# A new order of convolution units, evictions shared unit by unit, and a folded last chunk

## The chip, the cores and the metric

The kernel runs on one core of a Trainium2 chip. The metric is the device time of one execution in microseconds. Three runs of the kernel before took 3115.51, 3118.27 and 3122.56 us; the median is 3118.27.

The engines are TensorE (PE; matmuls), VectorE (DVE), ScalarE (ACT), GpSimd (POOL) and SyncE (SP, which issues the DMAs here). Each runs its own list of instructions in order and waits on semaphores.

## The reference

The input x has shape (8, 16, 112, 112): 8 images, 16 channels. Four residual stages follow each other, each on the group-normalised x (`_gn`: 8 groups of 2 channels, mean and variance over the group in the whole image):

```
x = x + L0(_gn(x))   # attention in windows of 4x4 pixels, 16 heads of width 1, projection
x = x + L1(_gn(x))   # 3x3 convolution, 16 -> 16 channels
x = x + L2(_gn(x))   # grid of 4 columns x 4 rows of 3x3 convolutions (below)
x = x + L3(_gn(x))   # 3x3 convolution of x rounded to 8 bits by one scale over all images
```

L2 is most of the work. Each of its 16 cells convolves up to three inputs of 16 channels and gives, after bias and relu, three outputs of 16 channels (right, up, down):

```
if col == 0:    ins = [input] if row == 0 else [outs[row - 1][-1]]
elif row == 0:  ins = [outs[row][0], outs[row + 1][1]]
elif row == 3:  ins = [outs[row][0], outs[row - 1][-1]]
else:           ins = [outs[row][0], outs[row + 1][1], outs[row - 1][-1]]
outs[row] = cell(W[col, row], b[col, row], ins)      # result: outs[-1][0]
```

L3's scale is the largest absolute value over all images, so L3 starts when the last image has left L2. In the attention of L0, each of the 16 queries of a window gets scores against 16 keys, a softmax over the keys and the weighted sum of the values.

## The kernel before

**Stages.** The program is written out as bodies m = -1 .. 7. Body m works on the grid of image m from cell (2,2) on, together with the first cells (columns 0, 1 and part of 2) of image m + 1, the attention of image m + 2 and conv1 (L1) of images m + 1 and m + 2. Ahead of body -1 (the early body, which has only the first cells of image 0) the attention of image 0 runs alone. Body 5 is the last with attention, body 6 (the late body) has convolutions alone, body 7 (the last) only the late cells of image 7. Then L3 runs for all images.

**Units.** A cell's outputs are computed unit by unit: 22U0 is cell (col 2, row 2), output up, first half of the image. `BODY` lists the cells, `units_of` takes all units of one cell one after the other. There are 68 in a body, 50 in the early, 18 in the last. In `conv_unit` (L846 for the last cell, L856, L870) a unit's matmuls go to two of four banks of PSUM. An input held as a "pair" (two inputs, 128 partitions) takes 48 matmul instructions at L856, one held as a "half" (64 partitions) 48 at L870. Cells of column 0 have a half alone, cells of rows 0 and 3 in the other columns a pair alone, the rest both. Unit k may start when unit k - 2 is emptied.

**Emptying** (eviction: bias and relu from PSUM into the input tiles of later cells). ScalarE does it in L706, four quarters per unit of 32x784 elements (or 32x392 twice, into a half). In cells that `SHARED_MID` names, which are (0,0) to (0,3), ScalarE takes two quarters and VectorE two (L1058, `empty`). The second half of an output emptied, SyncE sends its rows to the neighbouring partitions ("halos"): two DMAs for a pair (L497, L498), six for a half (L462 to L470). A unit's first use waits for them.

**Side steps** stand at fixed units, in tables: `PE_FIRST/MID/BEFORE` (attention's qkv L817 and projection L827, conv1 L783, the matmuls of means and variances L760, L765), `ACT_*` (copy of qkv L687, exponential L692), `SP_*` (loads, sends of the normalised input, store of a finished image). FIRST is body -1, BEFORE body 5, MID the bodies between. Both engines run their list in order, so a side step that must wait holds the units behind it.

**VectorE** in a body: the attention in 14 steps ("j"): `scores` (L1071 to L1083), `weigh` (L1095 to L1102), `residual` (L1110) after each projection; `add_conv1` (with the second normalising, L1046); `finish` of an image (L1267, added to the stream and measured); `move_stream`; `turn` at the end, with the statistics for the next image. Its evictions stand at fixed places: cell (0,0) after weigh 4, (0,1) after weigh 5, (0,2) after weigh 6, then `finish`, and (0,3) between scores 8 and weigh 7.

**First attention.** For image 0 a chunk's scores lie with the keys outermost, and TensorE sums over the 16 keys by matmuls with the identity (L890, `first_sums`): once the exponentials ("den"), once the weighted values ("num"). VectorE weighs (L1164), divides (`first_divide`, L1171, L1176) and adds the residual. There are 7 chunks.

## Time and profile before

| | us |
|---|---|
| median of three runs | 3118.27 |
| the profiled run | 3120.86 |
| its span, first to last instruction | 3119.1 |
| TensorE (PE) busy | 2786.1 (89%) |
| VectorE (DVE) busy | 2299.9 (74%) |
| ScalarE (ACT) busy | 2011.4 (64%) |
| mean granted clock of TensorE | 0.964 |

On the chain of waits that ended last TensorE has 70% of the span, VectorE 15%, ScalarE 10%. A row of the profile names the line of the kernel, the engine, the operation, output<-inputs and how often; a bracket at its end is the time that the engine was idle before it and what ended that. "Granted clock" 1.00 is 2.4 GHz, 0.50 is 1.2 GHz; there is nothing between the two but means over a stretch. An end of a matmul is modelled, so lengths of TensorE are best read from start to start.

### The profile page before, as it was taken

What the parts mean: (1) busy time and instruction counts of PE and PEld (TensorE: products, weight loads), DVE (VectorE), ACT (ScalarE), POOL (GpSimd) and SP (SyncE); (2) the same over time, 40 slices, a digit from 0 to 9 for tenths busy, and PEclk for the clock granted to TensorE, in tenths of its full rate; (3) what the DMA queues carried; (4) which work ended last, traced back from release to release, by engine and by line L of the source; (5) the groups of instructions that cost most, each with busy time, mean ns of one, the idle gap of its engine ahead of it and who ended that gap; (6) DMA issues with size and microseconds to landing.
All of it is one profiled execution on the core that took longest, in us unless ns stands there. A gap on an engine that the chain in (4) does not pass through costs nothing.

```text
span 3119.1 us, 84833 instructions
## 1 busy us (share of the span) xinstructions
PE 2786.1 (89%) x39155; PEld 1185.7 (38%) x39155; DVE 2299.9 (74%) x2105; ACT 2011.4 (64%) x2318; POOL 23.5 (1%) x68
## 2 busy tenths in 40 slices
PE   4755899989998899989998999989998989889976
PEld 3742333333333333333433343333333333333333
DVE  8969985899688986889598987899599961240135
ACT  1107976766767676766776776767776775766524
POOL 0000000000000000000000000000000000000000
PEclk9877999999999999999999999999999999999998
DMA  1014656586667667675657766685657664775566
GB/s 63 11 21 63 84 79 91 72 111 89 85 84 95 94 84 99 80 105 79 84 84 92 102 89 90 86 113 74 94 74 99 90 88 64 94 107 73 79 89 181
DMA packets 37555, 268.00 MB, mean 86 GB/s; under 512 B 19280, under 2 KB 19920, under 8 KB 24784
## 3 DMA queue, kind: packets, MB, share of 16 engines
q1 hardware_dynamic: 37008, 261.77, 59.6%
q8 instruction: 308, 5.05, 0.9%
q10 hardware_dynamic: 192, 0.80, 0.2%
q14 instruction: 47, 0.39, 0.1%
HBM read 22.54 MB, written 12.04 MB: 11 GB/s over the span
## 4 chain that ended last, share of the span: by engine, by line
PE 70%; DVE 15%; ACT 10%; issue 3%; SPq 1%; DMA 1%; POOL 0%; ACTq 0%; POOLq 0%; DVEq 0%
PE conv_banks L856 43%; PE conv_banks L870 20%; ACT pair L706 5%; ACT half L706 4%; DVE pair L1058 2%; DVE half L1058 2%; PE side_banks L817 2%; PE stat_bank L827 1%; PE side_banks L783 1%; ACT scores L692 1%; PE conv_banks L954 1%; DMA half<-half 1%; DVE scores L1073 1%; DVE score_max L1081 1%; DVE scores L1071 1%
## 5 line engine op out<-in xcount | busy, mean ns | idle before, releaser
L706 ACT ACTIVATE pair<-conv_banks,b_cells 32x784 f32<-32x784 f32 x1316 | 1213.0, 922 | 586.9 <-PE conv_banks L870 520.0
L856 PE MATMUL conv_banks<-pair,w_cells 128*32 128x392 f32 x17664 | 1538.1, 497 | 25.2 <-issue 11.6
L870 PE MATMUL conv_banks<-half,w_cells 64*32 64x392 f32 x18432 | 880.2, 508 | 143.8 <-ACT pair L706 60.7
L856 PEld LDWEIGHTS conv_banks<-pair,w_cells 128*32 128x32 f32 x17664 | 559.6, 109 | 948.0 <-issue 904.3
L706 ACT ACTIVATE half<-conv_banks,b_cells 32x392 f32<-32x392 f32 (+1 forms) x780 | 520.4, 667 | 172.7 <-PE conv_banks L870 133.9
L870 PEld LDWEIGHTS conv_banks<-half,w_cells 64*32 64x32 f32 x18432 | 337.4, 107 | 666.6 <-issue 620.8
L1058 DVE TENSOR_SCALAR half<-conv_banks,b_cells 32x392 f32<-32x392 f32 (+1 forms) x180 | 114.4, 636 | 326.5 <-PE conv_banks L870 168.4
L1058 DVE TENSOR_SCALAR pair<-conv_banks,b_cells 32x784 f32<-32x784 f32 x220 | 227.5, 1034 | 109.3 <-PE conv_banks L870 99.1
L1071 DVE TENSOR_TENSOR scores<-qkv 128x1792 f32<-128x1792 f32 x98 | 197.8, 2019 | 71.8 <-ACT qkv L687 71.5
L692 ACT ACTIVATE scores<-scores 128x1792 f32<-128x1792 f32 x104 | 176.7, 1699 | 78.5 <-DVE scores L1155 46.1
L1097 DVE TENSOR_TENSOR scores<-scores,qkv 128x1792 f32<-128x1792 f32 x98 | 198.4, 2025 | 3.4
L1073 DVE TENSOR_TENSOR scores<-scores,rel_bias_sb 128x1792 f32<-128x1792 f32 x98 | 198.4, 2025 | 3.3
L1083 DVE TENSOR_TENSOR scores<-scores,score_max 128x1792 f32<-128x1792 f32 x98 | 198.4, 2025 | 3.3
L1100 DVE TENSOR_REDUCE score_max<-scores 128x112 f32<-128x1792 f32 x98 | 197.9, 2020 | 3.4
L1081 DVE TENSOR_REDUCE score_max<-scores 128x112 f32<-128x1792 f32 x98 | 197.9, 2020 | 3.4
L1095 DVE TENSOR_REDUCE softmax_sum<-scores 128x112 f32<-128x1792 f32 x98 | 197.2, 2012 | 0.4
L687 ACT ACTIVATE qkv<-side_banks 128x672 f32<-128x672 f32 x56 | 40.9, 731 | 122.3 <-PE side_banks L817 92.5
L1046 DVE TENSOR_SCALAR half<-stream,norm 32x784 f32<-32x784 f32 x128 | 87.1, 680 | 3.1 <-DVE norm L1012 0.2
L1098 DVE RECIPROCAL softmax_sum<-softmax_sum 128x112 f32<-128x112 f32 x98 | 82.8, 845 | 0.0
L846 PE MATMUL conv_banks<-pair,w_cells 128*32 128x392 f32 x768 | 70.0, 515 | 12.5 <-issue 11.7
L817 PE MATMUL side_banks<-att,w_qkv_sb 128*128 128x224 f32 x294 | 68.0, 369 | 9.1 <-DVE att L1031 9.1
L827 PE MATMUL stat_bank<-att,w_proj_sb 128*128 128x112 f32 x448 | 65.8, 291 | 10.7 <-DVE stream L1110 10.7
(107 smaller groups left out, 1042.3 us busy)
## 6 DMA issues: line engine op xcount, KB each, us to landing
pair<-pair SPq DMA_DIRECT2D x384, 391.9 KB, 8.6
half<-half SPq DMA_DIRECT2D x348, 192.4 KB, 5.6
x_block<-in_xa SPq DMA_DIRECT2D x8, 784.0 KB, 11.0
stream<-in_xs SPq DMA_DIRECT2D x8, 784.0 KB, 10.5
x_scratch<-stream SPq DMA_DIRECT2D x7, 784.0 KB, 6.9
pair<-x_scratch SPq DMA_DIRECT2D x7, 784.0 KB, 14.2
out_dram<-pair SPq DMA_DIRECT2D x4, 1120.0 KB, 5.3
half<-half SPq DMA_DIRECT2D x174, 7.1 KB, 4.7
```

Of the source, the lines that this page charges most:

```text
L692: nc.scalar.activation(e, e, ACT.Exp).then_inc(exp_done, 1)
L706: done = nc.scalar.activation(dst, src, ACT.Relu, bias=b_ap)
L856: done = nc.tensor.matmul(conv_ps[32 * q:32 * q + 32, n + b, 0:QN], w, P[row][:, QG * s + BG * (q // 2):QG * s + BG * (q // 2 + 1), BX * ( ...
L870: done = nc.tensor.matmul(conv_ps[32 * q:32 * q + 32, n + h, 0:QN], w_all[rows, at:at + 32], T[rows, QG * u + BG * (q // 2):QG * u + BG * ...
L1058: done = nc.vector.tensor_scalar(dst, src, b_ap, 0.0, ALU.add, ALU.max)
L1071: ch.inc(nc.vector.tensor_tensor(e4, q, key, ALU.mult))
L1073: ch.inc(nc.vector.tensor_tensor(e, e, relb[:].unsqueeze(1).to_broadcast([BP, SW, WPX * WPX]), ALU.add))
L1081: ch.inc(nc.vector.tensor_reduce(m[:], ea, AX.X, ALU.max))
L1083: nc.vector.tensor_tensor(ea, ea, row_max(m), ALU.subtract).then_inc(scores_ready, 1)
L1095: side.inc(nc.vector.tensor_reduce(den[:], ea, AX.X, ALU.add))
L1097: side.inc(nc.vector.tensor_tensor(e4, e4, v, ALU.mult))
L1100: side.inc(nc.vector.tensor_reduce(mx[:], ea, AX.X, ALU.add))
```

## The change

- The list of cells is replaced by a list of units, `ORDER`, in which units of different cells alternate. A star marks units of the late cells. The early body runs those without a star, the last body those with one.
- VectorE's share of the evictions is given unit by unit: `VEC_MID` names 16 units at three places of VectorE's list (after weigh 4, after scores 7, after weigh 6), `VEC_LATE` 36 units of body 6, `VEC_LAST` 6 units of body 7. `finish` goes behind scores 10, `move_stream` behind weigh 13 (behind scores 2 in the early body).
- All tables of side steps get other places.
- In the early body `add_conv1` goes ahead of the first scores.
- In the first attention the last chunk's weighted values are added up by VectorE in four halving steps instead of by TensorE, and the division is split into `first_invert` and `first_apply`, placed ahead of the next weighing. The wait of the cleared tiles (GpSimd) is for one sum less.
- The first image's two normalised inputs are written half by VectorE, half by ScalarE.

```
-BODY = [((3, 0), 1), ((2, 2), 1), ((3, 1), 1), ((2, 3), 1), ((0, 0), 0), ((3, 2), 1), ((0, 1), 0), ((3, 3), 1),
-        ((0, 2), 0), ((1, 0), 0), ((0, 3), 0), ((1, 1), 0), ((1, 2), 0), ((2, 0), 0), ((1, 3), 0), ((2, 1), 0)]
-EARLY_BODY = [x for x in BODY if not x[1]]
-LATE_BODY = [x for x in BODY if x[1]]
...
+ORDER = """
+22U0* 22U1* 22D0* 22D1* 30D0* 30D1* 22R0* 22R1* 23U0* 23U1* 31D0* 31D1* 00D0 00D1 23R0* 00R0 23R1*
+32D0* 32D1* 00R1 01D0 01D1 01R0 01U0 01U1 33R0* 33R1* 02U0 02U1 01R1 02D0 10D0 02D1 02R0 02R1 10D1
+10R0 10R1 03U0 03U1 11U0 11D0 11D1 11U1 11R0 11R1 03R0 03R1 12D0 12D1 20D0 12U0 12U1 12R0 12R1 20D1
+20R0 20R1 13U0 13U1 13R0 13R1 21D0 21U0 21D1 21U1 21R0 21R1
+"""
...
+UNITS = units(ORDER)
+UNITS_F = [unit(t) for t in ORDER.split() if t[4:] != "*"]
+UNITS_L = [unit(t) for t in ORDER.split() if t[4:] == "*"]
...
+PE_MID = {0: [("qkv", 1, 0)], 4: [("proj", 0, 0), ("qkv", 2, 0)], 12: [("proj", 1, 0)], 13: [("qkv", 3, 0)],
+          19: [("proj", 2, 0)], 20: [("qkv", 4, 0)], 39: [("proj", 3, 0), ("qkv", 5, 0)],
+          47: [("proj", 4, 0), ("qkv", 6, 0)], 52: [("proj", 5, 0)], 56: [("proj", 6, 0)],
+          58: [("mean1", 0, 0)], 59: [("var1", 0, 0), ("mean0", 0, 1)], 60: [("var0", 0, 1)],
+          62: [("qkv", 0, 1)], 63: [("conv1", 0, 1)], 64: [("conv1", 1, 1)], 65: [("mean2", 0, 1)],
+          66: [("var2", 0, 1)]}
...
+PE_BEFORE = {0: [("qkv", 1, 0)], 4: [("proj", 0, 0), ("qkv", 2, 0)], 12: [("proj", 1, 0)], 13: [("qkv", 3, 0)],
+             19: [("proj", 2, 0)], 20: [("qkv", 4, 0)], 39: [("proj", 3, 0), ("qkv", 5, 0)],
+             47: [("proj", 4, 0), ("qkv", 6, 0)], 52: [("proj", 5, 0)], 56: [("proj", 6, 0)],
+             58: [("mean1", 0, 0)], 59: [("var1", 0, 0)], 63: [("conv1", 0, 1)], 64: [("conv1", 1, 1)],
              65: [("mean2", 0, 1)], 66: [("var2", 0, 1)]}
...
+ACT_MID = {0: [("qkv", 1, 0), ("exp", 1, 0)], 3: [("exp", 2, 0)], 5: [("qkv", 2, 0)], 6: [("exp", 3, 0)],
+           10: [("exp", 4, 0)], 14: [("qkv", 3, 0)], 16: [("exp", 5, 0)], 18: [("exp", 6, 0)],
+           24: [("qkv", 4, 0)], 25: [("exp", 7, 0)], 39: [("exp", 8, 0)], 41: [("qkv", 5, 0)],
+           43: [("exp", 9, 0)], 45: [("exp", 10, 0)], 48: [("qkv", 6, 0)], 49: [("exp", 11, 0)],
+           52: [("exp", 12, 0), ("exp", 13, 0)], 61: [("qkv", 0, 1)], 62: [("exp", 0, 1)]}
...
+SP_FIRST = {0: [("xb", 1), ("input", 0)], 30: [("xa", 2)], 38: [("conv1", 1)], 40: [("xb", 2)],
+            47: [("input", 1)]}
+SP_MID = {49: [("x3", -1), ("xa", 2)], 59: [("conv1", 1)], 62: [("xb", 2)], 65: [("input", 1)]}
+SP_BEFORE = {49: [("x3", -1)], 59: [("conv1", 1)], 65: [("input", 1)]}
+SP_LATE = {49: [("x3", -1)]}
+SP_LAST = {4: [("last", 0)], 13: [("last", 1)], NL - 2: [("last", 2)]}
...
+VEC_FIRST = {}
+VEC_MID = {("w", 4): "31D1 00D0 00D1 23R0",
+           ("s", 7): "01D0 01D1 01R0 01U0 01U1",
+           ("w", 6): "02U0 02U1 01R1 02D0 10D0 02D1 02R0"}
+FINISH_AT = ("s", 10)
+MOVE_AT_FIRST, MOVE_AT = ("s", 2), ("w", 13)
+VEC_LATE = """22U0 22D0 22D1 30D0 22R0 22R1 23U0 31D0 31D1 00D0 00D1 23R0 32D1 00R1 01D0 01D1 01R0 01U0 01R1 02D0
+10D0 02D1 02R0 02R1 10R0 10R1 03U0 11U0 11D1 11R0 11R1 03R0 12D0 12R0 12R1 13U1"""
+VEC_LAST = """22D1 30D1 31D0 31D1 23R1 32D1"""
+
+SHARED_FIRST, SHARED_MID = [[u for text in at.values() for u in units(text)] for at in (VEC_FIRST, VEC_MID)]
+SHARED_LATE, SHARED_LAST = units(VEC_LATE), units(VEC_LAST)
...
+                act.wait_ge(norm_sems[1 + which]["norm_ready"], 1)
+                for q in range(2, NQ):
+                    lo = QG * (q % 2)
+                    for xh in range(2):
+                        at = slice(32 * swapped(q, xh), 32 * swapped(q, xh) + 32)
+                        done = nc.scalar.activation(
+                            S[INPUT[1]][64:96, lo:lo + QG, 1 + BX * xh:1 + BX * (xh + 1)],
+                            X[at, :, BX * xh:BX * (xh + 1)], ACT.Identity, bias=nm[at, 3:4], scale=nm[at, 2:3])
+                    done.then_inc(c_own, 1)
+                act.wait_ge(c_own, (which + 1) * 2)
...
+                last = k == WROWS - 1
+                if k >= 1 and not last:
                     first_num(k - 1)
-                if k >= 2:
+                if k >= 2 and not last:
                     side_step(-2, "proj", k - 2)
                 pe.wait_ge(exp_done, SUBS * (k + 1))
...
+            side_step(-2, "proj", WROWS - 3)
             first_num(WROWS - 2)
-            first_num(WROWS - 1)
...
+                alone = not (isinstance(i, int) and i == 0)
+                for q in range(NQ if alone else 2):
...
+            def empty(m, mine):
+
+                for cell, o, u in mine:
+                    k = units_in(m).index((cell, o, u))
...
+            def first_fold(k, n):
+
+                dve.wait_ge(first_weighted, k + 1)
+                first.wait()
+                e = first_chunk_E[k % 3]
+                first.inc(nc.vector.tensor_tensor(e[:, 0:n], e[:, 0:n], e[:, n:2 * n], ALU.add))
...
+                    if 1 <= k < WROWS - 1:
+                        first_invert(k - 1)
+                        first_apply(k - 1)
+                    if k < WROWS - 1:
+                        first_weigh(k)
+                    if 2 <= k < WROWS - 1:
                         residual(0, k - 2)
-                first_divide(WROWS - 1)
-                residual(0, WROWS - 2)
+                k = WROWS - 1
+                first_invert(k - 1)
+                residual(0, k - 2)
+                first_weigh(k)
+                first_fold(k, 8)
+                first_apply(k - 1)
+                for n in (4, 2, 1):
+                    first_fold(k, n)
+                first_invert(k)
+                first_apply(k)
+                residual(0, k - 1)
...
+            def other_work(m, at):
+
+                early = isinstance(m, int) and m < 0
+                empty(m, units((VEC_FIRST if early else VEC_MID).get(at, "")))
+                if at == FINISH_AT and not early:
+                    finish(m, m)
+                if at == (MOVE_AT_FIRST if early else MOVE_AT):
+                    move_stream(m + 1)
...
+            def late_body(m):
+
+                mine, end = shared_in(m), units_in(m).index((LAST, RIGHT, 1))
+                before = [u for u in mine if m == B - 1 or units_in(m).index(u) < end]
+                if m < B - 1:
+                    add_conv1(m + 1)
+                empty(m, before)
+                finish(m, m)
+                empty(m, mine[len(before):])
+                if m < B - 1:
+                    move_stream(m + 1)
...
+                if early:
+                    add_conv1(m + 1)
                 scores(i, 0, side, E[:, 0], mx)
-                add_conv1(m + 1)
+                other_work(m, ("s", 0))
+                if not early:
+                    add_conv1(m + 1)
+                other_work(m, ("c1", 0))
                 for j in range(NSUB):
                     if j % SUBS == 0 and j // SUBS + 1 < WROWS:
                         normalise_chunk(i, j // SUBS + 1)
                     if j + 1 < NSUB:
                         scores(i, j + 1, side, E[:, (j + 1) % 2], mx)
-                    if not early and j == 7:
-                        empty(m, [(0, 3)])
+                        other_work(m, ("s", j + 1))
                     weigh(i, j)
-                    if not early and j == 4:
-                        empty(m, [(0, 0)])
-                    if not early and j == 5:
-                        empty(m, [(0, 1)])
-                    if not early and j == 6:
-                        empty(m, [(0, 2)])
-                    if not early and j == 6:
-                        finish(m, m)
-                    if j == 9:
-                        move_stream(m + 1)
+                    other_work(m, ("w", j))
```

## Rows read from the trace of the kernel before

**Rows 1.** Windows by stage: length, busy us of PE, PEld, DVE, ACT, POOL; granted clock, DMA.

```profile
247.70:531.50 283.80, 242.22 (x3464) 97.53 (x3464) 230.13 (x191) 218.66 (x257) 1.65 (x3) 0.93 0.56 78
531.50:2254.20 1722.70, 1631.62 (x24070) 657.11 (x24070) 1453.21 (x1286) 1230.62 (x1415) 8.23 (x15) 0.99 0.66 90
1910.30:2254.20 343.90, 325.22 (x4822) 131.07 (x4814) 290.70 (x258) 246.13 (x283) 1.65 (x3) 1.00 0.67 91
2254.20:2609.30 355.10, 328.59 (x4816) 130.25 (x4810) 280.26 (x242) 244.99 (x283) 1.10 (x2) 0.97 0.63 85
2609.30:2932.90 323.60, 306.42 (x4611) 116.16 (x4612) 53.17 (x64) 216.26 (x262) 0.00 (x0) 0.99 0.66 87
2932.90:3051.60 118.70, 100.78 (x1344) 41.91 (x1344) 33.98 (x36) 33.67 (x40) 1.59 (x6) 0.91 0.64 97
```

**Rows 2.** Groups by line and shape, one middle body: busy, mean ns, idle before and releasers.

```profile
L856 PE MATMUL conv_banks<-pair,w_cells 128*32 128x392 f32 x2208 | 192.3, 496 | 2.5 <-ACT half L706 1.3 <-issue 0.7 <-DVE pair L1058 0.5
L706 ACT ACTIVATE pair<-conv_banks,b_cells 32x784 f32<-32x784 f32 x164 | 151.2, 922 | 68.7 <-PE conv_banks L870 60.9 <-PE conv_banks L856 5.9
L870 PE MATMUL conv_banks<-half,w_cells 64*32 64x392 f32 x2312 | 107.8, 500 | 15.5 <-ACT pair L706 6.9 <-DVE half L1058 6.3 <-ACT pair L703 1.3
...
L1058 DVE TENSOR_SCALAR pair<-conv_banks,b_cells 32x784 f32<-32x784 f32 x28 | 29.0, 1034 | 7.1 <-PE conv_banks L870 6.7
...
L1046 DVE TENSOR_SCALAR half<-stream,norm 32x784 f32<-32x784 f32 x17 | 11.6, 680 | 0.4
L817 PE MATMUL side_banks<-att,w_qkv_sb 128*128 128x224 f32 x42 | 9.4, 359 | 0.0
...
L827 PE MATMUL stat_bank<-att,w_proj_sb 128*128 128x112 f32 x56 | 8.0, 286 | 0.0
...
L783 PE MATMUL side_banks<-half,w_conv 64*32 64x392 f32 x96 | 4.4, 490 | 0.0
```

**Rows 3.** Timeline of TensorE in the same body: start, length, what, idle before.

```profile
1926.07 4.20 PE L856 MATMUL conv_banks<-pair,w_cells 128*32 128x392 f32 x48
...
1932.35 4.20 PE L856 MATMUL conv_banks<-pair,w_cells 128*32 128x392 f32 x48
...
2025.96 4.34 PE L870 MATMUL conv_banks<-half,w_cells 64*32 64x392 f32 x96 [0.36 <-issue]
...
2053.56 5.60 PE L870 MATMUL conv_banks<-half,w_cells 64*32 64x392 f32 x96 [4.53 <-DVE half L1058]
...
2064.02 16.20 PE L856 MATMUL conv_banks<-pair,w_cells 128*32 128x392 f32 x192 [0.20 <-DVE pair L1058]
```

**Rows 4.** Timeline of VectorE in the same body, at the evictions of unit (0,2).

```profile
2035.58 2.02 DVE L1071 TENSOR_TENSOR scores<-qkv 128x1792 f32<-128x1792 f32 x1
...
2050.91 5.13 DVE L1058 TENSOR_SCALAR half<-conv_banks,b_cells 32x392 f32<-32x392 f32 x8
```

**Rows 5.** Timeline of body 5 at conv1, TensorE's and SyncE's rows.

```profile
2557.81 3.04 SPq L462 DMA_DIRECT2D half<-half  x1
...
2572.91 4.18 PE L783 MATMUL side_banks<-half,w_conv 64*32 64x392 f32 x48 [7.68 <-DMA half<-half]
```

**Rows 6.** Timeline of TensorE in the late body: a stall without a releaser.

```profile
2797.05 1.50 PE L870 MATMUL conv_banks<-half,w_cells 64*32 64x392 f32 x10 [4.41 <-issue]
```

**Rows 7.** Timeline of TensorE in the last body.

```profile
3013.59 6.83 PE L856 MATMUL conv_banks<-pair,w_cells 128*32 128x392 f32 x48 [6.22 <-issue]
...
3040.51 11.05 PE L846 MATMUL conv_banks<-pair,w_cells 128*32 128x392 f32 x96 [11.66 <-issue]
```

**Rows 8.** Timeline at the end of the first attention, VectorE and TensorE.

```profile
174.35 6.92 PE L890 MATMUL conv_banks<-scores,identity 128*128 128x224 f32 x32
...
181.30 3.89 DVE L1164 TENSOR_TENSOR scores<-scores,qkv 128x3584 f32<-128x3584 f32 x1 [8.91 <-PE conv_banks L890]
...
193.46 0.39 DVE L1176 TENSOR_TENSOR att<-conv_banks,pair 128x224 f32<-128x224 f32 x1 [3.84 <-PE conv_banks L890]
```

**Rows 9.** Timeline of VectorE at the end of the early body's attention.

```profile
461.90 0.45 DVE L1110 SCALAR_TENSOR_TENSOR stream<-stat_bank,b_proj_sb,stream 128x224 f32<-128x224 f32 x1 [8.54 <-PE stat_bank L827]
```

More of the change, by code:

```diff
@@ L105, in strips_of, with unit, units, starts @@
     return (u, u + 2) if has_single(col, row) else (2 * u, 2 * u + 1)
-BODY = [((3, 0), 1), ((2, 2), 1), ((3, 1), 1), ((2, 3), 1), ((0, 0), 0), ((3, 2), 1), ((0, 1), 0), ((3, 3), 1),
-        ((0, 2), 0), ((1, 0), 0), ((0, 3), 0), ((1, 1), 0), ((1, 2), 0), ((2, 0), 0), ((1, 3), 0), ((2, 1), 0)]
-EARLY_BODY = [x for x in BODY if not x[1]]
-LATE_BODY = [x for x in BODY if x[1]]
-def units_of(body):
-    return [(cell, o, u) for cell, late in body for o in cell_outs(*cell) for u in range(2)]
-UNITS_F, UNITS, UNITS_L = units_of(EARLY_BODY), units_of(BODY), units_of(LATE_BODY)
+ORDER = """
[4 more added lines that the diff above has]
+"""
+def unit(text):
+    return (int(text[0]), int(text[1])), "RUD".index(text[2]), int(text[3])
+def units(text):
+    return [unit(t) for t in text.split()]
+UNITS = units(ORDER)
+UNITS_F = [unit(t) for t in ORDER.split() if t[4:] != "*"]
+UNITS_L = [unit(t) for t in ORDER.split() if t[4:] == "*"]
 NF, NB, NL = len(UNITS_F), len(UNITS), len(UNITS_L)
 NS = NF + (B - 1) * NB + NL
-def body_of(m):
-    return (EARLY_BODY if m < 0 else LATE_BODY if m == B - 1 else BODY) if isinstance(m, int) else BODY
 def units_in(m):
-    return units_of(body_of(m))
+    return (UNITS_F if m < 0 else UNITS_L if m == B - 1 else UNITS) if isinstance(m, int) else UNITS
+def starts(m, k):
+    done = units_in(m)
+    return done[k][0] not in [cell for cell, _, _ in done[:k]]
 def unit_base(m):
@@ L153, in count_halos @@
             wrote(m, "input", INPUT)
-        for (cell, late) in body_of(m):
-            need[m, cell] = [(key, n[key]) for key in in_places(*cell)]
-            for o in cell_outs(*cell) if cell != LAST else []:
+        for k, (cell, o, u) in enumerate(units_in(m)):
+            if starts(m, k):
+                need[m, cell] = [(key, n[key]) for key in in_places(*cell)]
+            if u == 1 and cell != LAST:
                 wrote(m, (cell, o), out_place(*cell, o))
-        if m == -1:
-            n_first = dict(n)
     return need
@@ L226, in n_shared @@
 def n_shared(m, end):
-    return sum(cell in shared_in(m) for cell, _, _ in units_in(m)[:end])
+    return sum(done in shared_in(m) for done in units_in(m)[:end])
 def vec_value(m, k):
-    ahead, per = n_shared(-1, NF), sum(cell in SHARED_MID for cell, _, _ in UNITS)
+    ahead, per = n_shared(-1, NF), len(SHARED_MID)
     if not isinstance(m, int):
@@ L704, in empty @@
                     return
-                for dst, src, b_ap in unit_operands(k, cell, o, u, range(2 if cell in shared_in(m) else NQ)):
+                for dst, src, b_ap in unit_operands(k, cell, o, u, range(2 if (cell, o, u) in shared_in(m) else NQ)):
                     done = nc.scalar.activation(dst, src, ACT.Relu, bias=b_ap)
@@ L880, in body @@
                         side_step(m + d, kind, j)
-                    if cell == (0, 0) and cell != seen:
+                    if cell == (0, 0) and starts(m, k):
                         wait_halos(pe, m, "input")
-                    conv_unit(m, k, cell, o, u, cell != seen).then_inc(conv_done, 1)
-                    seen = cell
+                    conv_unit(m, k, cell, o, u, starts(m, k)).then_inc(conv_done, 1)
             def first_sums(kind, k, done_sem):
@@ L1048, in normalise_stream @@
                             nm[at, 2:3], nm[at, 3:4], ALU.mult, ALU.add)
-                    done.then_inc(c_ready, 1)
-            def empty(m, cells):
-                for k, (cell, o, u) in enumerate(units_in(m)):
-                    if cell not in cells:
-                        continue
+                    done.then_inc(c_ready, 1 if alone else 2)
+            def empty(m, mine):
+                for cell, o, u in mine:
+                    k = units_in(m).index((cell, o, u))
                     dve.wait_ge(conv_done, unit_base(m) + k + 1)
@@ L1336, in _ @@
             body(B - 3)
-            body(B - 2)
-            body(B - 1)
+            late_body(B - 2)
+            late_body(B - 1)
             dve.wait_ge(main_chain, B * MAIN_CHAIN)
```

105 lines of the change are left out of this document (37 added, 68 removed).

## The prediction, made before the changed kernel had run

> **What bounds the kernel now.** The windows by stage come first [rows 1]. The five middle bodies (one body is one image's 68 units) take 1722.7 us, 344.5 each; in the one shown TensorE is busy for 325.2 of 343.9, VectorE for 290.7, ScalarE for 246.1. So TensorE sets the pace there, and what can be won are its gaps. The same body by line and shape [rows 2] prices them: idle before the convolution's matmuls is 2.5 + 15.5 = 18.0, released by evictions of ScalarE and VectorE. TensorE's rows in order of time [rows 3] give clean prices: a unit with both inputs takes 6.28 from start to start (1926.07 to 1932.35), one with a pair alone 4.04 (16.20 for four), one with a half alone 2.1 to 2.2 (4.34 for two). A body has 28, 18 and 20 of these and two of the last cell at about 4.1: 175.8 + 72.7 + 42 + 8.2 = 298.7. Side steps cost 9.4 + 8.0 + 4.4 [rows 2] less some overlap, so a body without a gap is some 320. The other 24 are waits (18.0), half units started at 2.23 after a wait instead of 2.09, and loss of clock: after the wait of 4.53 two half units take 5.60 instead of 4.34 [rows 3].
>
> Why the waits stand where they do: two units share four banks, so unit k needs the eviction of k-2. A pair's eviction costs ScalarE 4 x 0.92 = 3.7, or with VectorE on two quarters about 2.1 (2 x 1.03) [rows 2]. The old order runs the short half units in blocks of four to six, each shorter than its eviction. And VectorE must be there: it ended an attention step (scores 8.1, weighing 7.2; 15.3 from 2035.58 to 2050.9) before it could begin on unit (0,2) [rows 4], which is the wait of 4.53.
>
> **The change, part by part.**
>
> *Order and evictions of a middle body.* TensorE's work is the same; only waits move. VectorE takes 16 units a body instead of 20, so 8 quarters go to ScalarE: +7.4 there, which has 98 idle, and -8 on VectorE. I ran the order by hand with these prices, from the body's start. VectorE begins the body's second step about 5 before it, since conv1 and its statistics stand two units and one unit earlier. Its first stop (after weighing 4) then comes at -5 + 77 = 72; TensorE finishes that stop's first unit, 31D1, at 70. This costs waits of 0.6, 0.35 and 0.25. At the second stop (after scores 7) VectorE is ready at 108.2 and TensorE ends its first unit at 107.5: waits 0.9, 0.3, 0.35. At the third (after weighing 6) VectorE is ready at 127.2 and the unit ends at 129.9, so it is VectorE that waits, 2.7. Then 1.25 behind the last cell (it is emptied only when both halves are done, as before) and 0.2 to 0.35 five times. Later: 1.3 at the fourth projection (VectorE's residual ends at 163.6, TensorE is there at 162.4) and 1.15 at 12D0. Between blocks the half units now stand among units of 4.04 and 6.28, during which ScalarE's 3.7 is hidden. Together 7.7, against 18.0. What was hidden and could become late: the seventh projection, at 260; VectorE's last weighing, the stream's move (now behind it) and a residual end at 258.9. That cover is 1.4 thin. To the 320 I add 7.7, 1 for conv1 (below) and 3.5 for the slower start after a wait: 332, or 12.5 less per body, 62.6 for five. Bounds: with no wait left it would be 320 (-24); if each of the three stops cost what one costs today (4.5 and 1.3 of clock), 332 + 17 = 349 (+5). I take 332, since the hand run stands on rows for every duration.
>
> *A rule against it.* ScalarE evicts 32x784 in 0.922 us, VectorE in 1.034 [rows 2]. The Trainium skill (ScalarE: Activation LUTs, Rules for kernel authors) says the opposite, that relu belongs on VectorE; by that, giving 8 quarters back to ScalarE would lose. The trace disagrees for this shape. And by either price the sum stays, because ScalarE is not the bound.
>
> *conv1 two units earlier.* Its halos are sent after the input is normalised, behind the second variance step, which moves up two units also; those are pair units (4.04), the ones it passes are long (6.28), so conv1 has some 4.5 less time after the normalising. Before, it starts with no wait (idle 0.0, L783 [rows 2]); after, SyncE takes this send ahead of two pair sends that stood before it. I take 1; bounds 0 and the 7.7 seen in body 5. In body 5 conv1's sends went out from 2557.81, right behind the pair sends of 13R1, and landed 15.1 later; TensorE waited 7.68 [rows 5]. The new table lets SyncE stand at conv1 three units earlier and places conv1 17 to 18 behind the variance step instead of 16.6, so I let this wait go. Body 5: 355.1 to 329.5, or -25.5 (waits as in the others -12.5; the wait at conv1, a second one behind it and their slow clock -13). Bounds -8 (halos stay late) and -34.
>
> *The late body (image 6).* No attention runs, VectorE takes 36 units instead of 20. By hand from 31D1 to 11U0: 92.4 against 82.8 of work; the largest waits are 1.8 and 1.5 at 01R1 and 02D0, when VectorE still adds and measures the finished image, and 1.2 behind the last cell. That gives 298.7 + 9.6 + 2. Not all of before's excess are evictions: a stall of 4.41 has no releaser [rows 6] and I leave half of such stalls in. 323.6 to 312.6: -11, bounds 0 and -18.
>
> *The last body.* TensorE waits 6.22 before 32D0 and then runs that pair part in 6.83 instead of 4.2 [rows 7]: the pair send of 23U stood behind a load of the scratch stream. Now 23U is four units ahead of 32D0 and that load goes out later. What is late next is 31D's half send, with the 8.1 of 23R and the 4.1 of 32D's own pair part before it; it needs about 11.6 and just fits. -8, bounds 0 and -9. The 11.66 before the last cell stays.
>
> *First attention.* VectorE waits 8.91 for the sixth chunk's sum over keys and 3.84 for the weighted sum [rows 8]; TensorE had three blocks of sums to run there, the first in 6.92. The fold replaces the last block by four VectorE additions of 3360 elements in all: up to 3.9, the price of the 3584-element multiply beside it [rows 8]. New path: sum of keys at 177 (its wait now ends when att 4 is applied, 168), weighing to 182.4, fold and apply to 187, reciprocal and product to 189.0, where the last product ended at 193.85: -4.9, and -0.4 for the residual behind it, which no longer meets TensorE's queue: -5.3. Dividing the normalising by two engines takes 4 of 8 instructions of 0.68 [rows 2] off VectorE but adds 4 of about 0.92 on ScalarE (an estimate, from its evictions of that shape), whose sends follow them: 5.4 becomes 3.7 to the last halo, -1.7. conv1 before the first scores: a further -5 for TensorE, since its sums no longer stand behind 8.1 of scores. The first conv unit could so start at 236 instead of 247.7 [rows 1]; yet ScalarE, in its order, stands at the third exponential until VectorE's scores are there, and VectorE's own chain has gained only some 6. So of 12 about 6 count.
>
> *The early body.* Its 50 units are 42 + 48.5 + 113 of work at the prices above, with side steps 223; it takes 283.8 [rows 1], since ScalarE empties everything. In the new order two of the half units and 10D, 10R stand between longer ones. By hand VectorE, 14 steps of 15.3, becomes the pace: attention ends at 444 (453.4 before, where VectorE then waited 8.54 for TensorE [rows 9]); projection 6 at 445, then 65 of work to the end at 511. I take 512 against 531.5: -19.5 with the part before. Bounds -8 and -24.
>
> **Sum.** 19.5 + 62.6 + 25.5 + 11 + 8 = 126.6 from the profiled run's 3120.9 (span 3119.1): 2994. The median of the runs shown is 2.6 below that run. For waits that such a hand run doesn't see (about half a microsecond a body) I add 5: 2997.
>
> **Rivals.**
> 1. VectorE is the second bound. The cover of 1.4 at the last projection is gone if anything makes VectorE late, and then every lateness is paid by TensorE. For it: 290.7 - 8 busy and the waits at norms stay. Against: the stops themselves ask for under 8. Half of the middle gain, two thirds elsewhere: 3120.9 - 31 - 43 = 3047.
> 2. Halos late at conv1: six bodies at 4 to 5 and 1.3 of clock: +30, 3027. For: the wait of 7.68. Against: the queue is empty when the send goes out.
> 3. Slower: VectorE comes late at all three stops. Unit k+2 waits on its half, and SyncE, in order, holds every later halo. The price of one late stop is on record: 4.53 and 1.3. It decides from 18 a body (126.6 over seven), which is 6 a stop; at 7 a stop the time is 3120.9 - 127 + 147 = 3141. For: VectorE was late at (0,2). Against: the hand run has it 2.2 late, 0.7 late and 2.7 early.
> 4. The order changes nothing since halos, not evictions, release the units: against it, the releasers [rows 2] are evictions, and DMA is none of them.
>
> The clock: TensorE is granted 1.00 in the body shown and 0.93 in the early one [rows 1]. The Trainium skill (TensorE: Matmul & The Clock Gate, Part 1) has idle time throttle the clock to half; the 5.60 after 4.53 agrees. By it, the short waits of the new order lose no clock, as the sum above has it too, and those of rival 3 do.
>
> **How the numbers follow.** Forecast 0.72, rival 1 0.12, rival 2 0.09, rival 3 0.05, rival 4 0.02. Own range of the forecast 2970 to 3025 (the bounds of the parts, with several at one side). The range to hold 8 in 10 reaches into rivals 1 and 2: 2968 to 3043. About 0.2% (6 us) is what a measurement can tell here: faster 0.93, same 0.02, slower 0.05.
>
> **What would show it.** Middle bodies near 332, with no wait of TensorE over 2; VectorE's evictions at the three stops begin within 3 of their unit's end; conv1 of body 5 with no DMA wait; 32D0 in the last body without its 6.22; the early body ending near 512. Wrong it would be if bodies stayed at 340 or more, above all with the wait at projections 3 or 6, or at conv1.

## The result, and the profile after

The changed kernel takes 3032.27 us (median of four runs, 3028.12 to 3042.12), 0.9731 of the kernel before (95% interval 0.9715 to 0.9747), 84.6 less than the 3116.89 that are the median of the kernel before with a fourth run (3113.03) counted in. The forecast was 2997, or 121 less. The time lies in the stated range of 2968 to 3043, but 35 above the forecast and outside the forecast's own range of 2970 to 3025. The profiled run has a span of 3030.6.

The windows by stage of the changed kernel (columns as in [rows 1]): the early body, the five middle bodies (0 to 4), the last of these alone (body 4), body 5, the late body, the last body.

```profile
236.30:516.20 279.90, 241.43 (x3475) 97.29 (x3477) 243.29 (x199) 220.78 (x259) 1.65 (x3) 0.94 0.57 79
516.20:2198.20 1682.00, 1627.84 (x24071) 660.22 (x24070) 1416.46 (x1256) 1265.80 (x1446) 8.25 (x15) 1.00 0.68 93
1862.10:2198.20 336.10, 325.90 (x4815) 131.75 (x4814) 283.31 (x252) 253.16 (x290) 1.65 (x3) 0.99 0.68 93
2198.20:2529.00 330.80, 322.91 (x4799) 129.71 (x4798) 265.19 (x231) 249.63 (x286) 1.10 (x2) 1.00 0.67 88
2529.00:2853.10 324.10, 307.30 (x4617) 117.34 (x4609) 87.55 (x102) 186.41 (x224) 0.00 (x0) 0.99 0.68 89
2853.10:2962.00 108.90, 97.22 (x1352) 35.98 (x1344) 13.29 (x16) 52.68 (x60) 1.59 (x6) 0.95 0.70 104
```

| stage | before | forecast | after |
|---|---|---|---|
| end of the early body | 531.5 | 512 | 516.2 |
| five middle bodies | 1722.7 | 1660 (332 each) | 1682.0 (339.8, 334.3, 332.8, 339.0, 336.1) |
| body 5 | 355.1 | 329.5 | 330.8 |
| late body | 323.6 | 312.6 | 324.1 |
| last body | 118.7 | 110.7 | 108.9 |

So the gain is missing in two stages: 22 in the middle bodies and 11.5 in the late body, which gained nothing in this trace. These are the groups of body 4 that answer to [rows 2]:

```profile
L891 PE MATMUL conv_banks<-pair,w_cells 128*32 128x392 f32 x2208 | 191.1, 496 | 1.9 <-ACT pair L741 1.4 <-DVE pair L1092 0.3 <-DVE half L1092 0.2
L741 ACT ACTIVATE pair<-conv_banks,b_cells 32x784 f32<-32x784 f32 x177 | 163.3, 922 | 51.3 <-PE conv_banks L905 42.6 <-PE conv_banks L891 6.4
L905 PE MATMUL conv_banks<-half,w_cells 64*32 64x392 f32 x2304 | 108.5, 501 | 5.4 <-DMA half<-half 2.5 <-ACT pair L741 1.0 <-issue 0.8
...
L1092 DVE TENSOR_SCALAR pair<-conv_banks,b_cells 32x784 f32<-32x784 f32 x16 | 16.5, 1034 | 10.1 <-PE conv_banks L905 8.1 <-PE conv_banks L891 1.8
```

The wait of 18.0 before the convolution's matmuls is now 7.3. VectorE's three stops there, and TensorE's rows that answer to [rows 3, 4]:

```profile
1932.55 7.77 DVE L1092 TENSOR_SCALAR half<-conv_banks,b_cells 32x392 f32<-32x392 f32 x12
...
1968.42 5.13 DVE L1092 TENSOR_SCALAR half<-conv_banks,b_cells 32x392 f32<-32x392 f32 x8
...
1993.72 2.09 DVE L1092 TENSOR_SCALAR pair<-conv_banks,b_cells 32x784 f32<-32x784 f32 x2 [6.31 <-PE conv_banks L905]
```

```profile
1989.80 5.13 PE L905 MATMUL conv_banks<-half,w_cells 64*32 64x392 f32 x80 [2.55 <-DMA half<-half]
...
2028.71 1.12 PE L862 MATMUL stat_bank<-att,w_proj_sb 128*128 128x112 f32 x8 [1.45 <-DVE stream L1144]
...
2078.53 4.19 PE L891 MATMUL conv_banks<-pair,w_cells 128*32 128x392 f32 x48 [1.36 <-ACT pair L741]
```

The first unit of the first stop, 31D1, ends at 1930.83 and that of the second, 01D0, at 1967.62; VectorE is 1.7 and 0.8 late (forecast 2 and 0.7). The fourth projection waits 1.45 (1.3), 12D0 1.36 (1.15). At the third stop VectorE waits 6.31 for 02U0 (forecast 2.7), because that unit itself is late: TensorE stood 2.55 for a DMA, and its 48 matmuls and 32 of the next unit's then took 5.13, where 96 take 4.34 in [rows 3]. The wait of 4.53 in front of the same unit before the change [rows 3] is back with another releaser. The waits of all five middle bodies (time in total, how often, the longest):

```profile
PE conv_banks L891 <- ACT pair L741: 10.0, 8, 1.4
PE conv_banks L905 <- issue: 8.4, 6, 3.1
PE conv_banks L905 <- DMA half<-half: 7.6, 3, 3.1
PE conv_banks L905 <- ACT pair L741: 5.1, 5, 1.0
PE conv_banks L891 <- issue: 4.8, 4, 1.7
PE conv_banks L905 <- DVE half L1092: 4.3, 13, 0.5
PE stat_bank L862 <- DVE stream L1144: 3.1, 3, 1.5
```

Evictions have 19.4 in these rows, 4 a body. The 13.2 of "issue" (no releaser in the trace) and the 7.6 of DMA were not among the forecast's waits. In the late body (TensorE) the same two stand:

```profile
2644.04 8.59 PE L881 MATMUL conv_banks<-pair,w_cells 128*32 128x392 f32 x78 [3.17 <-issue]
...
2701.35 2.49 PE L905 MATMUL conv_banks<-half,w_cells 64*32 64x392 f32 x48 [2.07 <-DMA half<-half]
...
2713.61 1.53 PE L905 MATMUL conv_banks<-half,w_cells 64*32 64x392 f32 x7 [3.52 <-issue]
```

**What the two are.** 02U0 needs the halos of 01D. SyncE's rows around it:

```profile
1964.75 0.51 SPq L521 DMA_DIRECT2D pair<-pair  x1
...
1968.50 0.51 SPq L521 DMA_DIRECT2D pair<-pair  x1
...
1973.58 0.83 SPq L486 DMA_DIRECT2D half<-half  x1
...
1979.22 0.93 SPq L494 DMA_DIRECT2D half<-half  x1
```

The send of 01D's half starts at 1973.58 and its last part goes out at 1979.22, behind the pair sends of 32D (1964.75) and 00R (1968.50); the landing of the last part was at 1989.71, 16.1 after the first issue. The windows of that stretch and three others show why (the last three columns are granted clock, DMA share and GB/s):

```profile
1969.00:1987.20 18.20, 17.11 (x288) 6.76 (x272) 17.52 (x19) 12.16 (x16) 0.00 (x0) 1.00 1.07 134
1990.50:1993.00 2.50, 2.50 (x40) 0.94 (x32) 0.00 (x0) 0.00 (x0) 0.00 (x0) 0.50 0.13 17
2080.00:2084.00 4.00, 4.00 (x68) 1.58 (x65) 3.70 (x4) 2.85 (x4) 0.00 (x0) 1.00 0.89 98
2632.90:2640.90 8.00, 7.71 (x136) 3.06 (x126) 5.07 (x6) 6.32 (x9) 0.00 (x0) 1.00 1.04 124
```

From 1969.0 to 1987.2 the 16 DMA engines are full (1.07; the view counts a packet whole where it starts, and with the packets cut at the window's ends it is 1.02). They are full also in the 8 us before the stall that ends at 2644.04 (1.04, or 1.01). That stall has no releaser, because the matmul behind it waits on no semaphore. The trace's DMA records have a second kind beside the sends: reads of instructions, 16,384 bytes each. One is on its engine from 2640.6 to 2642.4, and TensorE goes on at 2644.04; for the stall that ends at 2713.61 one runs from 2710.4 to 2712.2. After 500 us the changed kernel has 11 stalls over 0.6 us before a convolution's matmul that waits on nothing, 19.7 in all, and before 10 of them the DMA share over the 8 us ahead (packets cut at its ends) was 0.98 or more. The kernel before had 8, with 13.3; the 4.41 of [rows 6] is one.

The records don't name the engine that the instructions are for, but two counts do. The middle bodies have 190 such reads (number, MB, share of the 16 engines):

```profile
q8 instruction: 190, 3.11, 1.0%
```

That is one for every 253 of TensorE's 48,141 matmuls and weight loads there (windows above). The early body has one for every 257 (27 reads), the late body one for every 256 (36), while VectorE and ScalarE together have 14, 17 and 9 instructions to a read. And when TensorE's instructions are numbered in the order of their starts, those of its sequencer included, the instructions that follow the 11 stalls all come 193 or 194 places behind a multiple of 256; so do those that follow the 8 stalls of the kernel before. In each of the 19 a read had ended 1.4 to 2.0 us earlier. TensorE therefore stands where the next piece of its own program is missing.

Of the clock the same windows show: behind the wait of 2.55 it is granted 0.50 (1.2 GHz, 1990.5 to 1993.0), behind the wait of 1.36 at 12D0 it is 1.00 (2.4 GHz, 2080 to 2084). The length of a wait does not decide it alone: behind a stall of 2.10 that ends at 824.50 the clock was 0.50, behind one of 3.07 that ends at 1656.68 it stayed at 1.00:

```profile
1656.68:1660.09 3.41, 3.41 (x82) 1.62 (x83) 1.18 (x2) 1.19 (x2) 0.00 (x0) 1.00 0.02 5
```

### The profile page after: what moved, and what is told of

Read it like the earlier page. It is cut to its first block, busy times and chain, and to the rows that moved or that the text cites. A ratio compares the mean times of both kernels' runs of the same rounds, so it can differ in the third digit from the quotient of the medians.

```text
span 3030.6 us, 84780 instructions
## 1 busy us (share of the span) xinstructions
PE 2764.6 (91%) x39123; PEld 1174.9 (39%) x39123; DVE 2268.4 (75%) x2083; ACT 2050.0 (68%) x2344; POOL 23.5 (1%) x68
## 4 chain that ended last, share of the span: by engine, by line
PE 53%; DVE 27%; issue 5%; ACT 5%; DMA 2%; SPq 1%; POOL 0%; POOLq 0%; DVEq 0%
PE conv_banks L891 33%; PE conv_banks L905 14%; DVE scores L1107 3%; DVE score_max L1115 3%; ACT pair L741 3%; DVE scores L1105 3%; DVE half L1092 3%; DVE score_max L1134 3%; DVE scores L1131 3%; DVE softmax_sum L1129 3%; DMA half<-half 2%; DVE half L1081 2%; DVE pair L1092 2%; PE conv_banks L881 2%; PE side_banks L818 1%
## 5 line engine op out<-in xcount | busy, mean ns | idle before, releaser
L741 ACT ACTIVATE pair<-conv_banks,b_cells 32x784 f32<-32x784 f32 x1384 | 1276.7, 922 | 451.1 <-PE conv_banks L905 374.5
L741 ACT ACTIVATE half<-conv_banks,b_cells 32x392 f32<-32x392 f32 (+1 forms) x730 | 487.0, 667 | 184.3 <-PE conv_banks L905 121.8
L905 PEld LDWEIGHTS conv_banks<-half,w_cells 64*32 64x32 f32 x18432 | 328.5, 106 | 587.2 <-issue 555.9
L1092 DVE TENSOR_SCALAR pair<-conv_banks,b_cells 32x784 f32<-32x784 f32 x152 | 157.2, 1034 | 285.8 <-PE conv_banks L905 236.7
L1092 DVE TENSOR_SCALAR half<-conv_banks,b_cells 32x392 f32<-32x392 f32 (+1 forms) x230 | 151.4, 658 | 84.1 <-PE conv_banks L905 60.2
L923 PE MATMUL conv_banks<-pair,identity 128*128 128x224 f32 x256 | 54.7, 376 | 24.9 <-DVE pair L1198 24.9
```

The costliest lines, as they stand in the source:

```text
L741: done = nc.scalar.activation(dst, src, ACT.Relu, bias=b_ap)
L905: done = nc.tensor.matmul(conv_ps[32 * q:32 * q + 32, n + h, 0:QN], w_all[rows, at:at + 32], T[rows, QG * u + BG * (q // 2):QG * u + BG * ...
L1092: done = nc.vector.tensor_scalar(dst, src, b_ap, 0.0, ALU.add, ALU.max)
```

## The experiments

Theory A: the DMA engines are full where the new order sends most, and TensorE then waits for halos and for its own instructions. Theory B, rival 1 of the prediction: VectorE is the second bound. All times are medians; a ratio is to the kernel before, run on the same chip.

**1. 00R's send behind 01D's (send_later).**

```
+ if (cell, o) == ((0, 0), RIGHT):
+     held_back = key; continue
  send_half(sp, key) if key[0] == "half" else send_pair(key)
+ if (cell, o) == ((0, 1), DOWN):
+     send_pair(held_back)
```

> One edit in SyncE's list: the pair send of 00R goes out behind the half send of 01D instead of ahead of it; no unit and no eviction moves. Theory A (the 16 DMA engines are full in this stretch, so 01D's halos come late to 02U0): the half send loses one pair send, some 6.6 us, from its queue, the wait of 2.0 to 3.1 at 02U0 and the half clock behind it (2.4 to 4.5 together in bodies 0, 2 and 4) go, 2 to 4 a body: 3032 falls to 3015 to 3025, and 02U0 shows no wait on a DMA. Theory B (VectorE is the second bound and pays for the missing gain): nothing changes, 3029 to 3035.

3013.33, ratio 0.9656 (0.9641 to 0.9671): 19 less by one send in another place, a little more than the 7 to 17 expected. 33R, then 02U0, in body 4 on TensorE:

```profile
1973.08 8.28 PE L886 MATMUL conv_banks<-pair,w_cells 128*32 128x392 f32 x96 [0.21 <-DVE pair L1097]
1982.50 4.22 PE L910 MATMUL conv_banks<-half,w_cells 64*32 64x392 f32 x96 [1.14 <-ACT pair L743]
```

Only the 1.14 behind the last cell is left at 02U0. The middle bodies are 339.1, 336.8, 331.7, 331.3, 330.9, 12 less together; the two that stay long have stalls without a wait of 3.70 at 01R1 and 3.34 at 02D0. Another 8.6 come from the late body (315.5), which varies by as much where nothing in it was changed (run 4).

**2. Pair sends of half the bytes (half_sends).**

```
+ n = HG if m >= 1 else G
- sp.dma_start(T[at:at + 16, 1:G], T[own + 16:own + 32, 0:G - 1])    # and its twin
+ sp.dma_start(T[at:at + 16, 1:n], T[own + 16:own + 32, 0:n - 1])
```

> From body 1 on each pair send moves 27 of its 55 rows, so half of the pair halos are left out of the computation; the number of sends and of instructions is the same. Theory A (DMA engines full, and what TensorE waits for without a releaser are its own instructions, read behind the sends): waits on DMAs and stalls without a releaser over 0.7 go in bodies 1 to 6; bodies 1 to 4 fall to 328 to 330 (-5 to -9 each), the late body to 310 (-14), the last body by up to 9: 2965 to 2995. If reading instructions is slow by itself, the stalls without a releaser stay (late body 320 or more) and only waits on DMAs go: 3005 to 3015. Theory B: 3025 to 3033.

2987.51, ratio 0.9576 (0.9562 to 0.9591). The kernel leaves out half of the pair halos from body 1 on. Its body 2 and its late body:

```profile
1186.60:1516.70 330.10, 322.86 (x4819) 130.64 (x4819) 283.33 (x252) 253.24 (x290) 1.65 (x3) 1.00 0.39 65
2504.80:2813.30 308.50, 300.11 (x4620) 114.90 (x4615) 87.55 (x102) 186.41 (x224) 0.00 (x0) 1.00 0.37 60
```

With a DMA share of 0.37 to 0.39 bodies 1 to 4 take 330.0 to 331.0 and the late body 308.5; after body 0 no stall without a wait is left. Theory A holds for both kinds of wait. The edit takes away bytes and also the long packets (12,312 bytes each instead of 25,080); run 6 parts the two.

**3. VectorE made lighter (light_vector).**

```
- nc.vector.tensor_tensor(ea, ea, row_max(m), ALU.subtract)
+ nc.vector.tensor_tensor(ea[:, 0:8], ea[:, 0:8], row_max(m)[:, 0:8], ALU.subtract)   # not in the early body
```

> In bodies 0 to 5 the subtraction of the row maximum works on 8 of 112 rows of scores (the rest is left out), which takes some 1.9 of 2.02 us off each of VectorE's 14 steps, 26 a body. Theory B (VectorE is the second bound): a body gains at least 6, half of what is missing against 332 and the waits at its stops: 3032 falls below 2995. Theory A: only waits on VectorE's rows go (about 1.4 at a projection, 0.3 to 1 at the first and second stop): 2 to 3 a body, 3012 to 3022, and waits on DMAs and stalls without a releaser stay or grow.

3031.0, ratio 0.9718 (0.9694 to 0.9742): no gain that can be told.

```profile
1861.40:2197.80 336.40, 325.15 (x4815) 130.49 (x4814) 259.52 (x252) 253.05 (x290) 1.65 (x3) 0.99 0.68 93
```

VectorE has 259.5 where it had 283.3, and body 4 is 336.4 against 336.1. The wait at the fourth projection is gone, but a unit later one of 1.15 for ScalarE stands in its place. Theory B falls, and theory A's 3012 to 3022 was too hopeful by that. Run 6 confirms it from the other side: there bodies of 330 go with 283.3 of VectorE's work.

**4. Fewer shared evictions in the late body (late_shares, and late_split with the sends of run 6).**

```
- VEC_LATE = """22U0 22D0 22D1 ... 13U1"""     # 36 units
+ VEC_LATE = """31D1 00D0 00D1 23R0 01D0 01D1 01R0 01U0 01U1 02U0 02U1 01R1 02D0 10D0 02D1 02R0"""
```

> In the late body VectorE takes the 16 units that it takes in a middle body instead of 36; ScalarE takes the rest. By the prediction's own reckoning (evictions bound this body, and the 36 are what takes waits away) the late body grows by 5 to 10 from its 324.0: 3037 to 3042. Theory A (this body is bound by its sends and by instructions read behind them): it stays within 4 of 324.0, 3028 to 3036.

> Pair sends split as in the last runs, and the late body's 36 shared evictions cut to the 16 of a middle body: the shares' own price, without the stalls that lay over it. With unsplit sends the cut moved the late body from 324.0 to 325.8 only, but waits on evictions of some 10 stood in its trace in place of other stalls. If these are the evictions' own, the late body grows by 6 to 10 from 308.8 and the time is 2990 to 2994; if evictions don't bound this body, it stays within 3 and the time is 2981 to 2987.

late_shares: 3033.2, 0.9719 (0.9706 to 0.9732), the late body 325.8 against 324.1: within 4, as theory A had it. But this body varies with unsplit sends: in old_first, conv1_behind, no_shares and light_vector, which change nothing in it, it took 316.3 to 320.4. What the shares are worth under these sends is therefore open, anything from 1.7 to 9.5. late_split: 2998.74, 0.961 (0.9596 to 0.9623); the late body is 322.8 against 308.4 to 308.8 in the three runs with 36 shared units and split sends. So the choice of these units is worth 14.0, more than expected. On TensorE in late_split:

```profile
2596.60 2.23 PE L905 MATMUL conv_banks<-half,w_cells 64*32 64x392 f32 x48 [1.99 <-ACT pair L741]
...
2629.76 0.91 PE L905 MATMUL conv_banks<-half,w_cells 64*32 64x392 f32 x8 [6.26 <-DVE pair L1092]
```

This one wait of 6.26 stands at 01R1, where split_only has one of 1.96: VectorE comes to its quarters of 02U0 only behind the finish of the image. The 16 units include 02U0 and 02U1, which the 36 leave to ScalarE, so some 4 of the 14 come from which units are shared and not from how many. The other long waits are for ScalarE.

**5. The order alone (no_shares).** `VEC_MID = {}`.

> The changed kernel with the middle bodies' 16 shared evictions given back to ScalarE (those of the late and last body stay): the new order alone. By the prices of the prediction: at the three stops ScalarE needs 4.9 and 3.7 a unit where TensorE needs 2.1 to 2.2; that leaves it 5, 9 and 10 behind, 24 a body, less some 4 of waits on DMAs and instructions that then are hidden: +15 to +20 in each of bodies 0 to 5, 3122 to 3152, about the time of the kernel before. If the gain is of the order alone (rival), the time stays below 3070.

3144.38, ratio 1.0087 (1.0072 to 1.0101). The new order without shares in these bodies is slower than the kernel before, which shares 20 units a body; the middle bodies take 354 to 362, as expected. What the old order would take with shares chosen unit by unit was not run. Its waits there:

```profile
PE conv_banks L903 <- ACT half L739: 48.8, 30, 2.6
PE conv_banks L889 <- ACT pair L739: 31.0, 23, 2.2
PE conv_banks L903 <- ACT pair L739: 23.1, 19, 2.0
```

**6. Pair sends in two pieces (send_split: with run 1's edit; split_only: without).**

```
- sp.dma_start(T[at:at + 16, 1:G], T[own + 16:own + 32, 0:G - 1])
- sp.dma_start(T[at + 16:at + 32, 0:G - 1], T[own:own + 16, 1:G])
+ for lo, hi in ((0, HG), (HG, G - 1)):
+     sp.dma_start(T[at:at + 16, lo + 1:hi + 1], T[own + 16:own + 32, lo:hi])
+     sp.dma_start(T[at + 16:at + 32, lo:hi], T[own:own + 16, lo + 1:hi + 1])
```

> On top of the later send of 00R: each pair send goes out as four DMAs of 27 or 28 rows instead of two of 55, with the same bytes. A packet of a pair send is 25,080 bytes and takes 3.4 us in the saturated stretch; it becomes half as long. If TensorE's instruction reads wait behind whole packets in front of them, its stalls without a releaser shorten to about half and the time falls by 4 to 12 from 3013: 3001 to 3009. If it is the bytes queued that count, the stalls stay and the time stays within 4 (3009 to 3017). If SyncE's extra issues (0.5 to 0.6 us each, two more a send) hold the half sends behind them, waits on DMAs grow: 3018 or more.

> The changed kernel with pair sends in four DMAs of half the rows, 00R's send in its place ahead of 01D's: which of the two edits of the last split took the stalls away. If the length of a packet is the cause, stalls without a releaser go here too, the late body comes to 310 or less, and only the wait on a DMA at 02U0 stays where 01D is behind 00R: 2984 to 2996. If the two edits are needed together, the late body stays above 315 and the time above 3000.

send_split 2984.38, 0.9574 (0.9561 to 0.9587), far beyond the 4 to 12 expected; split_only 2984.13, 0.9572 (0.9556 to 0.9587). The split alone does it; with it, 00R's place is worth nothing. split_only by stage (middle bodies, body 5, late, last) and its late body's waits:

```profile
518.30:2170.40 1652.10, 1615.31 (x24071) 653.21 (x24070) 1416.43 (x1256) 1264.88 (x1446) 8.23 (x15) 1.00 0.61 94
2170.40:2497.40 327.00, 319.67 (x4799) 128.79 (x4798) 265.07 (x231) 249.40 (x286) 1.10 (x2) 1.00 0.60 90
2497.40:2806.20 308.80, 301.34 (x4617) 114.92 (x4609) 87.56 (x102) 186.23 (x224) 0.00 (x0) 0.99 0.62 93
2806.20:2915.30 109.10, 98.14 (x1352) 36.09 (x1344) 13.29 (x16) 52.60 (x60) 1.59 (x6) 0.94 0.64 107
```

```profile
PE conv_banks L906 <- ACT pair L742: 2.4, 2, 2.0
PE conv_banks L906 <- DVE half L1093: 2.2, 4, 0.8
PE conv_banks L906 <- DMA half<-half: 1.3, 1, 1.3
```

Every middle body takes 330.0 to 330.8, the late one 308.8, and no stall over 0.6 without a wait is left anywhere behind 500 us. At the third stop of body 4 VectorE now waits 2.52 for 02U0, where 2.7 was forecast:

```profile
1967.58 4.20 DVE L1093 TENSOR_SCALAR pair<-conv_banks,b_cells 32x784 f32<-32x784 f32 x4 [2.52 <-PE conv_banks L906]
```

The page's row of pair sends in the changed kernel, and those in split_only (KB each, median us to landing):

```profile
pair<-pair SPq DMA_DIRECT2D x384, 391.9 KB, 8.8
```

```profile
pair<-pair SPq DMA_DIRECT2D x384, 199.5 KB, 5.2
pair<-pair SPq DMA_DIRECT2D x384, 192.4 KB, 6.0
```

A packet of 25,080 bytes took 3.35 us (median, late body), two of 12,768 and 12,312 took 1.48 and 1.40. The same bytes so need less of the engines (0.61 of a shorter stretch for 0.68), and a read waits behind shorter packets. Full engines alone do not stop TensorE: between 500 and 2990 us, 49 of its 278 reads in split_only begin behind 8 us with a share of 0.98 or more, and no stall follows. In the changed kernel 68 of 276 do, and 10 of the 11 stalls follow these. So the long packets are needed for a stall; whether a read then waits behind one of them or behind several the runs don't separate. The Trainium skill (DMA: Bandwidth & Descriptors, Queues, rings and completion order) says that a DMA engine takes turns between its queues by whole packets; the stalls that go with the packet's length agree. The Trainium skill (Perfetto Trace Analysis, What "DMA-bound" means) advises large descriptors for a kernel that is bound on DMA; here, where TensorE is busy for 91% of the span, halving the packets won 48 us.

**7. The same split in the kernel before (before_split).**

> The kernel before, with the same split of the pair sends and nothing else. Its trace had stalls without a releaser of about 7 in the five middle bodies, 8.5 in the late body and 4 in body 5, and 7.7 at conv1 on a half send behind two pair sends. If packets are the cause of these, 12 to 25 go: 3094 to 3106, and the late body falls from 323.6 to 312 to 315. The change is then worth 110 to 120 with packets that don't hold it up, close to the 121 that were predicted. If the split helps only where evictions stand close, the time stays within 6 of 3117.

3095.35, ratio 0.9928 (0.9915 to 0.994). Its late body falls from 323.6 to 310.7, its middle bodies only from 344.5 to 342.9. Between the two kernels with split sends the change is worth 111.2; their profiled runs by stage:

| stage | forecast | unsplit sends | split sends |
|---|---|---|---|
| first attention, early body | -19.5 | -15.3 | -13.0 |
| five middle bodies | -62.6 | -40.7 | -62.6 |
| body 5 | -25.5 | -24.3 | -22.9 |
| late body | -11 | +0.5 | -1.9 |
| last body | -8 | -9.8 | -7.2 |

**8. Parts of the start (old_first, conv1_behind).** The first sums the last chunk on TensorE again and divides in one piece; the second is

```
- if early:
-     add_conv1(m + 1)
  scores(i, 0, side, E[:, 0], mx)
- if not early:
-     add_conv1(m + 1)
+ add_conv1(m + 1)
```

> The changed kernel with the first attention's end as it was: the last chunk's weighted values summed by TensorE, the division in one piece behind the weighing. By the prediction the fold is worth 4.9 and 0.4 on VectorE's chain: the first convolution unit starts 5 later (241 to 242) and the time grows by about 5, 3034 to 3040. If the early body absorbs it (VectorE's 14 steps are not behind anything of this): 3029 to 3034.

> The changed kernel with the early body's add of conv1 behind its first scores, as before the change. By the prediction TensorE's first unit starts some 5 to 8 later (241 to 245), but as VectorE's chain is as long either way, the early body ends within 2 of 516.2 and the time stays within 4 of 3032. If the early units are paced by conv1's halos and not by VectorE, the early body ends 5 to 8 later: 3037 to 3041.

old_first 3036.02 (0.9722 to 0.9764), conv1_behind 3028.02 (0.9696 to 0.9726): both intervals overlap the changed kernel's, so the times are inconclusive. The traces say more: without the fold the first unit starts at 242.8, against 236.1 to 239.4 in the nine traces with the changed start, and the early body ends at 521.9, against 515.7 to 519.5. With the add behind the scores it starts at 241.0, and the early body still ends at 515.6, so this part of the change gains nothing.

**9. The best version (best):** runs 1, 6 and conv1_behind together.

> Later send of 00R, split pair sends, and the add of conv1 in the early body behind the first scores, as it was before the change. The last alone took about 4 off the changed kernel: if that was its own doing, 2978 to 2982 here against 2984; if it was only another place of the stalls, 2983 to 2987.

2981.78, ratio 0.9564 (0.9549 to 0.9579), the fastest here; the early body ends at 514.9 against 517.5 in send_split. Against send_split's own interval the 2.6 isn't settled.

## Why the prediction was right and wrong

- **Right: the evictions.** The hand run put the middle body at 332; with the DMA engines out of the way it is 330.4 (1652.1 / 5). The three stops and both later waits came within 0.3 of their forecast where a DMA didn't move them. That the gain with split sends on both sides is 62.6, to the digit, is chance: both kernels are some 1.6 a body below what the forecast started from and came to. Rival 3 and rival 1 are refuted, rival 1 by runs 3 and 6.
- **Wrong: "Together 7.7", the sum of a middle body's waits.** It priced 02U0 by evictions alone. The halos of 01D behind two pair sends were left out, though the same pattern, a half send right behind pair sends that landed 15.1 later, was read from [rows 5]. Rival 2 had the mechanism, but looked for it at conv1 alone, where TensorE waited for a DMA only twice in the middle bodies (0.62 in body 0, 0.95 in body 4). That the time is near its 3027 is luck. At 02U0 the waits were 3.08, 2.01 and 2.55 in bodies 0, 2 and 4, the first and the last with the half clock behind them. From 33R1 to 02D0 these bodies took 3.7, 1.2 and 4.3 longer than with split sends, and run 1 took the waits away.
- **Wrong: "I add 5" for what the hand run doesn't see, and "leave half of such stalls in" for [rows 6].** Stalls without a wait were 19.7 in all against 13.3, without the half clock behind some of them. They are TensorE's instructions, read behind long packets on full DMA engines (runs 2 and 6). Why the new order has more of them the runs don't show.
- **Wrong: the late body's -11.** The level (312.6) is near the 308.8 of split sends, but what the kernel before lost there was not evictions: split sends alone take it to 310.7. With the same sends the change wins 1.9 there. The 36 shares are worth 14 against 16 others (run 4); with those 16 the new order takes 322.8, which is 12.1 more than the old order with its 20.
- **Wrong in part: the clock.** The forecast had only rival 3's long waits cost clock; the waits of 2.55 and 3.08 at 02U0 did too, and the one of 2.01 there did not.
- **Right: body 5 and the last body.** 330.8 for 329.5, with no wait at conv1; 108.9 for 110.7, the 6.22 before 32D0 gone and 11.66 before the last cell left.
- **Start.** The first unit starts at 236.3, as the forecast allowed; the early body ends 4 later than forecast. The last product was put 4.9 earlier and came 3.4 earlier, since VectorE met a projection's wait of 3.28:

```profile
179.40 0.45 DVE L1144 SCALAR_TENSOR_TENSOR stream<-stat_bank,b_proj_sb,stream 128x224 f32<-128x224 f32 x1 [3.28 <-PE stat_bank L862]
...
190.09 0.39 DVE L1216 TENSOR_TENSOR att<-scores,pair 128x224 f32<-128x224 f32 x1
```

## What to carry to other kernels

When a reordering takes waits on engines away, ask next what it does to the transfers: list the sends between each producer and its first consumer, and price a consumer by the queue in front of its send, not by a send alone. A stall whose matmul waits on no semaphore is a question to the DMA records: look for a full DMA share ahead of it and a read of instructions that ends just before the engine goes on, and count the engine's instructions between two stalls. Then shorten the packets of bulk transfers before moving anything else; here that was worth 48 us (23 in the kernel before) where the whole search of an order had been worth 85. And take a stage that varies between runs from more than one trace before a few us of it are explained.

## What the hardware showed that was not expected

This program, written out in full, reads TensorE's instructions through DMA queues beside its data, 16,384 bytes for every 253 to 257 matmuls and weight loads. TensorE stood for up to 4.41 us at once when such a read came late, each time at the same place in a count of 256 of its instructions. Full engines were not enough for that: with packets of half the length no stall followed 49 reads behind full engines. SBUF to SBUF packets of 25,080 bytes move 7.5 KB per us on an engine, those of half the size 8.6 to 8.8 (late body of split_only). And a change of shares that is worth 14 us looked worth 1.7 in one pair of traces while other stalls stood in the same stage.
